# Gathered groups of a four-layer graph network: one matmul per edge column over the three bf16 parts side by side, summed by VectorE out of PSUM

## The chip, the cores and the metric

The kernel runs on one core of a Trainium2 chip. The metric is the time of one execution on the device in microseconds (us); lower is better. TensorE multiplies matrices into PSUM, VectorE does elementwise work and reductions, ScalarE activations, GpSimd (POOL) starts the indirect gathers, and SyncE (SP) starts the plain DMA transfers. [...]

## The reference

12500 nodes with 64 features, 200000 edges `src -> dst` sorted by `dst`, and four layers in a row, each followed by a residual and a layer norm:

```python
edge_index = jnp.stack([src, dst])
x = _layernorm(x + _L0_gnn_ref(x, edge_index, ...))            # graph attention, 4 heads
x = _layernorm(x + _L1_gnn_ref(x, edge_index))                 # standard deviation of the neighbours
x = _layernorm(x + _L2_gnn_ref(x, edge_attr_64, src, dst, ...))# messages with edge features, then an MLP
x = _layernorm(x + _L3_gnn_ref(x, edge_index, ...))            # four sage_conv in a row

def sage_conv(x, src, dst, Wl, bl, Wr):
    msg = x[src]
    agg = jax.ops.segment_sum(msg, dst, num_segments=N_NODES)
    deg = jax.ops.segment_sum(jnp.ones((src.shape[0], 1), x.dtype), dst, num_segments=N_NODES)
    agg = agg / jnp.maximum(deg, 1.0)
    return agg @ Wl.T + bl + x @ Wr.T
```

The core of each layer is a segment sum: for every node, the sum of the rows of its in-neighbours. The second layer needs the sums of x and of its square (128 columns), the four `sage_conv` those of 64, 32, 32 and 64 columns.

## The kernel before

Nodes are cut into 98 tiles of 128. There are seven passes over the graph: gat, dev, gine, sage1, sage2, sage3, sage4. Gat and gine gather every edge's row in f32. The other five (dev and the four sage passes) are "dense" passes with `parts` = 3: a float is split into three bf16 parts, which lie side by side in a table row of 3 x n columns (n = 128, 64, 32, 32, 64), and a sum over the three parts gives the f32 sum back.

A dense pass (`pass_dense`, once for TensorE and once for VectorE) sums in two ways:

- **Counted tiles.** For the first 49 destination tiles (KT = 49) the kernel has built, once, a matrix of edge counts per pair of tiles in DRAM (`counts`). `dense_unit` streams one destination tile's count blocks through the SBUF ring `RING` in pieces (`piece_loaded`, `piece_used`) and multiplies each 128x128 block with the rows of all source tiles, in two halves with a PSUM bank each (`ps_dense`): 98 matmuls a unit (in dev, whose tables are wider, the source tiles are taken in two sweeps, 49 matmuls a unit). Line 921 is that matmul; it already takes the three parts at once, 3 x n columns wide. VectorE's `take_dense` (lines 1740 to 1752) reduces the three parts out of PSUM into `DSUM` (L1746), waits for that reduce, and adds it to the accumulator (L1750).
- **Gathered groups.** The remaining edges, those of the higher destination tiles, are taken in 15 rounds per pass. A round (`cold_round`) has 8 slots, a slot is a group of 512 edges, 128 partitions by C = 4 edge columns. POOL gathers the rows of a slot with 4 indirect DMAs (L620) as soon as the slot's indices have been refilled (`take_indices`, L1695). A group touches one or more destination tiles t; each (group, tile) is a **pair**. For a pair VectorE writes a one-hot matrix of 128x512 (`hot`, L1700) into one of two buffers, and TensorE multiplies it with the gathered rows into one of two PSUM banks (`ps_pair`, L949): 4 edge columns times 3 parts, 12 matmuls of n columns that accumulate into the same n columns.

A gathered round is called from `cold_rounds` between two units; how many rounds stand behind which unit is a schedule computed on the chip (`TURNS`). The order on TensorE is written by hand: unit (both halves), then rounds, then the next unit. On VectorE it is `take_dense` of half 0, the rounds, `take_dense` of half 1.

Within a round the two engines run one pair apart. VectorE, for pair p: one-hot of p, wait for the matmuls of p-1 (`pair_agg`), add the sum of p-1 from PSUM to the accumulator of its tile (`add`, L1707), then swap the buffers. TensorE, for pair p: wait for the one-hot of p (`pair_hot`) and for the add of p-2 (`pair_acc`), which frees the PSUM bank. After every 7 units the last pair still in PSUM is added by `flush`, whose steps run on a chain semaphore (`step` waits for each), and then the node work of a block or two follows (`node_vector`, `node_tensor`: L1200, L685 and so on); TensorE goes on with the next unit afterwards.

`settle(eng)` is a semaphore increment that carries the wait ahead of it.

Of the kernel before, what the change touches and what calls it, by code (L numbers as in the profile page):

```python
# [25 lines left out]
C = 4  # L26
# [58 lines left out]
def build(nc, x, edge_attr, src_r, dst_r, dst_b, src_c, dst_c, w, out):  # L85
    ctx = ExitStack()
    with ctx:
        def sb(name, shape, dt=F32):
            return ctx.enter_context(nc.sbuf_tensor(name, shape, dt))

        def sem(name):
            return ctx.enter_context(nc.semaphore(name))
# [43 lines left out]
        xp_before = [sum(xp_loads[:k]) for k in range(len(passes))]  # L136

        table_done = sem("table_done")
        pair_hot, pair_agg, pair_acc = sem("pair_hot"), sem("pair_agg"), sem("pair_acc")
        piece_loaded = [sem(f"piece_loaded_{j}") for j in range(len(PIECES))]  # L140
        piece_used = [sem(f"piece_used_{j}") for j in range(len(PIECES))]
        xp_loaded, dense_read, dense_added = sem("xp_loaded"), sem("dense_read"), sem("dense_added")
# [94 lines left out]
        iota_f = arena(WIDE_ROW, at=5 * COLS + 4 * TB)  # L237

        DSUM = sb("DSUM", [P, 2, 2 * D])
        MOST = sb("MOST", [P, 2])  # L240
        FLAG = sb("FLAG", [P, 1])
        HOTS = sb("HOTS", [P, 2])
# [469 lines left out]
        def _(pe):  # L712
# [212 lines left out]
            def pass_dense(k):  # L925

                ps = passes[k]
                n, buf, row = ps["n"], ps["buf"], ps["row"]
                dev = ps["name"] == "dev"

                def cold_round(r):

                    pe.reg_add(arrived, arrived, 16 * C)
                    for s in range(SLOTS):
                        lo, hi = load_four(pe, spans, s, r * SLOTS + s)
                        pe.wait_ge(ps["gathered"][s], pe.snap(arrived, min_val=1, max_val=len(passes) * ROUNDS * 16 * C))
                        settle(pe)
                        with pe.Fori(lo, hi) as t:
                            pe.reg_add(seen, seen, 1)
                            count = pe.snap(seen, min_val=1, max_val=len(passes) * GROUPS * TILES)  # L940
                            pe.wait_ge(pair_hot, count)
                            settle(pe)
                            pe.wait_ge(pair_acc, count)
                            settle(pe)
                            hot = onehot_ring[:, bass.ds(pe.snap(turn, min_val=0, max_val=1024), GE)]
                            sums = ps_pair[:, bass.ds(pe.snap(bank, min_val=0, max_val=512), n)]
                            for c in range(C):
                                for q in range(3):
                                    last = pe.matmul(sums, hot[:, c * P:(c + 1) * P], buf[:, s, c, q * n:(q + 1) * n],  # L949
                                                     start=(c == 0 and q == 0), stop=(c == C - 1 and q == 2))  # L950
                            last.then_inc(pair_agg, 1)
                            pe.reg_alu(turn, turn, 1024, ALU.bitwise_xor)
                            pe.reg_alu(bank, bank, 512, ALU.bitwise_xor)

                r0 = pe.value_load(INFO[0:1, 0:1], min_val=0, max_val=ROUNDS - 1)
                if dev:
                    pe.wait_ge(chunk_read, CHUNKS + 2)
                    for q in range(2):
                        last = pe.matmul(ps_pair[:, 512 * q:512 * q + n], ZERO[:, :], ZEROS[:, 0:n], start=True, stop=True)
                    last.then_inc(pair_agg, 1)  # L960
                    for half in range(2):
                        pe.wait_ge(xp_loaded, 16 * (xp_before[k] + half + 1))
                        with pe.Fori(0, KT) as u:
                            dense_unit(k, u, u + half * KT, SRC_HALF)
                            if half == 0:
                                cold_rounds(pe, u, r0, cold_round)
                    return
                pe.wait_ge(xp_loaded, 16 * (xp_before[k] + xp_loads[k]))
                with pe.Fori(0, STEPS) as b:
                    with pe.Fori(0, TB) as r:  # L970
                        u = b * TB + r
                        dense_unit(k, u, u, TILES)
                        cold_rounds(pe, u, r0, cold_round)
                    node_tensor(pe, k, b * 2)
                    node_tensor(pe, k, b * 2 + 1)
# [275 lines left out]
        def _(ve):  # L1251
# [433 lines left out]
            def pass_dense(k):  # L1685
# [11 lines left out]
                def hot(cols, t):  # L1697
# [3 lines left out]
                                                   TBASE[:, bass.ds(t, 1)], COL[:, :].unsqueeze(1).broadcast_to([P, C, P]),  # L1701
                                                   ALU.subtract, ALU.is_equal)

                def add():

                    a = acc[:, bass.ds(ve.snap(prev, min_val=0, max_val=TILES), 1), :]
                    return ve.tensor_tensor(a, a, ps_pair[:, bass.ds(ve.snap(bank, min_val=0, max_val=512), n)].unsqueeze(1), ALU.add)  # L1707

                def cold_round(r):

                    for s in range(SLOTS):
                        g = r * SLOTS + s
                        lo, hi = load_four(ve, spans, s, g)
                        with ve.Fori(lo, hi) as t:  # L1714
                            ve.reg_add(pairs, pairs, 1)
                            count = ve.snap(pairs, min_val=1, max_val=len(passes) * GROUPS * TILES)
                            hot(g * C + C, t).then_inc(pair_hot, 1)
                            ve.wait_ge(pair_agg, count)
                            settle(ve)
                            ve.wait_ge(pair_acc, count)  # L1720
                            settle(ve)
                            add().then_inc(pair_acc, 1)
                            ve.reg_mov(prev, t)
                            ve.reg_alu(turn, turn, 1024, ALU.bitwise_xor)
                            ve.reg_alu(bank, bank, 512, ALU.bitwise_xor)
                        take_indices((s - 1) % SLOTS, g + (SLOTS - 1))

                def flush():

                    ve.reg_add(after, pairs, 1)  # L1730
                    count = ve.snap(after, min_val=1, max_val=len(passes) * GROUPS * TILES)
                    ve.wait_ge(pair_agg, count)
                    settle(ve)
                    ve.wait_ge(pair_acc, count)
                    settle(ve)
                    step(add())
                    settle(ve)
                    ve.reg_mov(prev, TILES)
# [23 lines left out]
                    take_indices(s, r0 * SLOTS + s)  # L1762
                if name == "dev":
                    with ve.Fori(0, STEPS) as b:
                        step.loop(b, per + 1)
                        with ve.Fori(0, TB) as r:
                            unit(b * TB + r, b * TB + r, True)
                        flush()
                        node_vector(ve, step, k, split, b, b + STEPS)
# [6 lines left out]
                    step.close(STEPS)  # L1776
                    return
                with ve.Fori(0, STEPS) as b:
                    step.loop(b, 2 * per + 1)
                    with ve.Fori(0, TB) as r:  # L1780
                        unit(b * TB + r, b * TB + r, True)
                    flush()
# [50 lines left out]
```

## Time and profile before

| | |
|---|---|
| median of 3 runs | 12794.58 us (12789.05 to 12804.66) |
| the profiled execution | 12813.53 us |
| its span on the core | 12811.7 us |
| mean granted TensorE clock | 0.668 of full speed |
| TensorE matmul busy | 7656.7 us (60%), 61727 matmuls |
| TensorE weight load busy | 5494.5 us (43%) |
| VectorE busy | 5118.7 us (40%) |
| ScalarE busy | 1761.8 us (14%) |
| POOL busy | 5615.3 us (44%) |
| passes with gathered groups of three parts | dev's from 5.86 ms, sage1 to sage4 from 9.2 ms to the end |

The busy shares are means over stages with different limits. PE is TensorE's matmul row, PEld its weight loads, DVE VectorE; an engine's name with a q behind it is its sequencer. An instruction is named by its line, as L949. "Idle before" is what the engine had no work for, and the arrow names what ended it; "issue" means that nothing in the profile did.

### The profile page before, as it was taken

How to read it: one execution, taken by the hardware profiler on the slowest of the kernel's cores; microseconds unless marked ns; L12 is line 12 of the kernel's file. 1: busy time of each engine (PE TensorE's matmuls, PEld its weight loads, DVE VectorE, ACT ScalarE, POOL GpSimd, SP SyncE). 2: the span in 40 equal slices, each digit the busy share in tenths (PEclk: the TensorE clock that was granted, in tenths of full speed). 3: DMA queues.
4: the chain of work that ended last, by engine and by line, in shares of the span. 5: the costliest groups of instructions: out<-in, count | busy, mean ns of one | idle time of the engine just before them, and what ended most of it. 6: DMA issues, size and time to landing. Idle time of an engine off the chain costs nothing.

```text
span 12811.7 us, 273411 instructions
## 1 busy us (share of the span) xinstructions
PE 7656.7 (60%) x61727; PEld 5494.5 (43%) x61728; DVE 5118.7 (40%) x13474; ACT 1761.8 (14%) x3566; POOL 5615.3 (44%) x5555
## 2 busy tenths in 40 slices
PE   5666666663665555556788444444566655455666
PEld 4555555552112222224455333444555544444566
DVE  4444545546544444443433222333322233322333
ACT  2333333331012222330000000000000000000000
POOL 4666555452000000005530577777654376554554
PEclk7777777776555555557889655566677766666777
DMA  2222222221001111115555322222455566655666
GB/s 59 66 63 63 64 62 61 61 59 36 20 40 54 66 70 70 70 80 169 150 169 176 75 51 56 56 58 58 121 189 173 198 206 232 217 183 199 203 216 202
DMA packets 977744, 1416.34 MB, mean 111 GB/s; under 512 B 540705, under 2 KB 649761, under 8 KB 970914
## 3 DMA queue, kind: packets, MB, share of 16 engines
q1 hardware_dynamic: 689858, 1130.79, 26.0%
q0 software_dynamic: 184832, 224.29, 9.0%
q10 hardware_dynamic: 102752, 58.62, 1.6%
q14 instruction: 281, 2.30, 0.1%
q8 instruction: 21, 0.34, 0.0%
HBM read 1197.73 MB, written 215.36 MB: 110 GB/s over the span
## 4 chain that ended last, share of the span: by engine, by line
PE 31%; issue 23%; DVE 14%; DVEq 14%; POOL 9%; DMA 6%; ACT 1%; SPq 1%; POOLq 0%; ACTq 0%
PE ps_turn L921 13%; POOL ARENA L620 9%; PE ps_turn L884 7%; PE ps_out L776 4%; DMA ARENA<-table_gat,idx 2%; DMA ARENA<-counts 2%; DVE onehots L1700 2%; DVEq L1714 2%; PE ps_pair L776 1%; DMA idx<-src_r 1%; DVEq L392 1%; PE ps_turn L692 1%; PE ps_pair L949 1%; DVE ARENA L1635 1%; DVEq L1630 1%
## 5 line engine op out<-in xcount | busy, mean ns | idle before, releaser
L620 POOL DMA_INDIRECT ARENA<-table_sage,idx x1920 | 1901.7, 990 | 1729.5 <-DVE idx L1695 1192.8
L921 PE MATMUL ps_turn<-ARENA 128*128 128x96 bf16 (+2 forms) x24010 | 2274.4, 262 | 543.0 <-DVE DSUM L1746 215.9
L921 PEld LDWEIGHTS ps_turn<-ARENA 128*128 128x128 bf16 x24010 | 1864.0, 106 | 948.7 <-issue 647.7
L884 PE MATMUL ps_turn<-ARENA 128*128 x3736 | 1515.8, 508 | 1219.5 <-issue 584.4
L620 POOL DMA_INDIRECT ARENA<-table_gat,idx x1568 | 1671.9, 1066 | 1188.1 <-issue 1131.0
L620 POOL DMA_INDIRECT ARENA<-table_gine,idx x1568 | 1541.2, 983 | 964.1 <-issue 950.1
L620 POOL DMA_INDIRECT ARENA<-table_dev,idx x480 | 481.8, 1004 | 2660.0 <-DVE idx L1695 2522.3
L1635 DVE TENSOR_SCALAR ARENA<-ARENA 128x784 f16 x1868 | 902.6, 483 | 1415.9 <-PE ps_turn L884 963.9
L949 PE MATMUL ps_pair<-ARENA,onehots 128*128 128x32 bf16 (+2 forms) x10140 | 699.7, 227 | 997.4 <-DVE ARENA L1707 868.6
L776 PE MATMUL ps_out<-ARENA,onehots 128*128 128x256 f32 (+1 forms) x3136 | 950.0, 472 | 517.7 <-DMA ARENA<-table_gine,idx 368.9
L884 PEld LDWEIGHTS ps_turn<-ARENA 128*128 x3736 | 389.1, 104 | 1959.0 <-issue 1863.2
L776 PE MATMUL ps_pair<-ARENA,onehots 128*128 128x256 f32 (+1 forms) x3136 | 882.5, 446 | 389.1 <-DMA ARENA<-table_gine,idx 303.4
L949 PEld LDWEIGHTS ps_pair<-ARENA,onehots 128*128 x10140 | 574.0, 117 | 1128.3 <-issue 1127.1
L776 PEld LDWEIGHTS ps_out<-ARENA,onehots 128*128 128x128 f32 x3136 | 724.1, 286 | 631.5 <-issue 555.5
L1073 ACT ACTIVATE ARENA<-ps_turn 128x784 f32 x784 | 645.4, 823 | 2112.9 <-PE ps_turn L902 2112.9
L1746 DVE TENSOR_REDUCE DSUM<-ps_turn 128x128 f32<-128x384 f32 (+2 forms) x588 | 230.0, 391 | 1756.2 <-PE ps_turn L921 1643.5
L1700 DVE SCALAR_TENSOR_TENSOR onehots<-DST,TBASE,COL 128x512 f32 x845 | 637.0, 754 | 640.0 <-issue 639.5
L776 PEld LDWEIGHTS ps_pair<-ARENA,onehots 128*128 128x128 f32 x3136 | 677.8, 269 | 493.9 <-issue 429.3
L1030 ACT ACTIVATE bigT<-ps_turn 128x896 f32<-128x896 f32 (+1 forms) x42 | 38.4, 915 | 3454.3 <-PE ps_turn L685 3454.3
L1450 DVE TENSOR_TENSOR ARENA<-ARENA,ps_out 128x261 f32 (+1 forms) x584 | 205.7, 354 | 761.8 <-PE ps_out L776 761.3
L1018 ACT ACTIVATE tmp<-COL,dst_in 128x128 bf16<-128x128 f32 x1568 | 495.3, 386 | 0.0
L776 PE MATMUL ps_out<-ARENA,tmp 128*128 128x256 f32 (+1 forms) x1536 | 417.2, 435 | 128.0 <-DVE tmp L1444 126.2
(298 smaller groups left out, 6850.4 us busy)
## 6 DMA issues: line engine op xcount, KB each, us to landing
ARENA<-counts SPq DMA_DIRECT2D x1470, 448.0 KB
counts<-ARENA SPq DMA_DIRECT2D x49, 3136.0 KB, 9.0
ARENA<-counts SPq DMA_DIRECT2D x490, 224.0 KB
ARENA<-dst_b SPq DMA_DIRECT2D x393, 256.0 KB
ARENA<-edge_attr SPq DMA_DIRECT2D x390, 128.0 KB, 2.5
ARENA<-table_sage,idx POOLq DMA_INDIRECT x1920
ARENA<-table_gat,idx POOLq DMA_INDIRECT x1568
ARENA<-table_gine,idx POOLq DMA_INDIRECT x1568
```

What stands on the lines that cost most here:

```text
L620: pool.indirect_dma_start(ps["buf"][:, s, c, 0:ps["row"]], None, ps["table"][:, :], bass.IndirectOffsetOnAxis(idx[:, s, c:c + 1], 0)).then ...
L776: last = pe.matmul(sums[:, 0:H * D if gat else n], lhs, rhs, start=(c == 0 and q == 0), stop=(c == C - 1 and q == parts - 1))
L884: last = pe.matmul(ps_turn[:, at:at + WIDE_ROW // 2], ring[:, 0:P], ring[:, P + q * (WIDE_ROW // 2):P + (q + 1) * (WIDE_ROW // 2)], start= ...
L921: last = pe.matmul(ps_dense[half][:, 0:n], RING[:, b, :], XP[:, b, :], start=(b == PIECE_AT[pieces[0]]), stop=(j == pieces[-1] and b == PI ...
L949: last = pe.matmul(sums, hot[:, c * P:(c + 1) * P], buf[:, s, c, q * n:(q + 1) * n], start=(c == 0 and q == 0), stop=(c == C - 1 and q == 2))
L1018: act.activation(distance[:, c * P:(c + 1) * P], COL[:, :], ACT.Abs, scale=-1.0, bias=dst_in[:, s % 2, c:c + 1]).then_inc(hot_distance, 1)
L1073: act.activation(to[:, :, c * CHUNK:(c + 1) * CHUNK].rearrange("p (q b) v -> p q b v", q=2), sums.rearrange("p q (b v) -> p q b v", v=CHUN ...
L1450: return ve.tensor_tensor(a, a, ps_sums[q][:, 0:n].unsqueeze(1), ALU.add)
L1635: ve.tensor_scalar(ring[:, P:P + WIDE_ROW], IOTA16, BASES[:, bass.ds(i * 4 + c, 1)], KEY[:, bass.ds(j, 1)], ALU.add, ALU.is_equal).then_in ...
L1700: return ve.scalar_tensor_tensor(ring, DST[:, bass.ds(cols, C)].unsqueeze(2).broadcast_to([P, C, P]), TBASE[:, bass.ds(t, 1)], COL[:, :].u ...
L1714: with ve.Fori(lo, hi) as t:
L1746: ve.tensor_reduce(DSUM[:, half, 0:n], ps_dense[half][:, 0:3 * n].rearrange("p (q v) -> p v q", q=3), X_AXIS, ALU.add).then_inc(dense_read, 1)
```

## The change

In `cold_round` of TensorE the inner loop over the three parts goes. One matmul per edge column takes the slot's whole row, 3 x n columns, into 3 x n columns of the PSUM bank (at most 384 of 512). VectorE gets a new step `join`, a reduce over the three parts out of PSUM into a new SBUF tile `PAIR_SUM`, with a semaphore `pair_sum` on which the add then waits; the add reads `PAIR_SUM`. The flush gets the same two steps, as two links of its chain. In dev the banks' opening with zeros covers all three parts.

```diff
@@ TensorE, cold_round
-                            sums = ps_pair[:, bass.ds(pe.snap(bank, min_val=0, max_val=512), n)]
+                            sums = ps_pair[:, bass.ds(pe.snap(bank, min_val=0, max_val=512), 3 * n)]
                             for c in range(C):
-                                for q in range(3):
-                                    last = pe.matmul(sums, hot[:, c * P:(c + 1) * P], buf[:, s, c, q * n:(q + 1) * n],
-                                                     start=(c == 0 and q == 0), stop=(c == C - 1 and q == 2))
+                                last = pe.matmul(sums, hot[:, c * P:(c + 1) * P], buf[:, s, c, :], start=(c == 0), stop=(c == C - 1))
                             last.then_inc(pair_agg, 1)
@@ TensorE, dev: the banks are opened with zeros
                     for q in range(2):
-                        last = pe.matmul(ps_pair[:, 512 * q:512 * q + n], ZERO[:, :], ZEROS[:, 0:n], start=True, stop=True)
+                        for part in range(3):
+                            last = pe.matmul(ps_pair[:, 512 * q + part * n:512 * q + (part + 1) * n], ZERO[:, :], ZEROS[:, 0:n], start=True, stop=True)
@@ VectorE
+        PAIR_SUM = sb("PAIR_SUM", [P, 2 * D])
+                def join():
+
+                    parts = ps_pair[:, bass.ds(ve.snap(bank, min_val=0, max_val=512), 3 * n)]
+                    return ve.tensor_reduce(PAIR_SUM[:, 0:n], parts.rearrange("p (q v) -> p v q", q=3), X_AXIS, ALU.add)
+
                 def add():

                     a = acc[:, bass.ds(ve.snap(prev, min_val=0, max_val=TILES), 1), :]
-                    return ve.tensor_tensor(a, a, ps_pair[:, bass.ds(ve.snap(bank, min_val=0, max_val=512), n)].unsqueeze(1), ALU.add)
+                    return ve.tensor_tensor(a, a, PAIR_SUM[:, 0:n].unsqueeze(1), ALU.add)
@@ VectorE, cold_round
                             ve.wait_ge(pair_acc, count)
                             settle(ve)
+                            join().then_inc(pair_sum, 1)
+                            ve.wait_ge(pair_sum, count)
+                            settle(ve)
                             add().then_inc(pair_acc, 1)
@@ VectorE, flush
                     ve.wait_ge(pair_acc, count)
+                    settle(ve)
+                    step(join())
                     settle(ve)
                     step(add())
```

## Rows read from the trace of the kernel before

**Rows 1.** The page: the chain that ended last, by engine and by line.
```profile
PE 31%; issue 23%; DVE 14%; DVEq 14%; POOL 9%; DMA 6%; ACT 1%; SPq 1%; POOLq 0%; ACTq 0%
PE ps_turn L921 13%; POOL ARENA L620 9%; PE ps_turn L884 7%; PE ps_out L776 4%; DMA ARENA<-table_gat,idx 2%; DMA ARENA<-counts 2%; DVE onehots L1700 2%; DVEq L1714 2%; PE ps_pair L776 1%; DMA idx<-src_r 1%; DVEq L392 1%; PE ps_turn L692 1%; PE ps_pair L949 1%; DVE ARENA L1635 1%; DVEq L1630 1%
```

**Rows 2.** Groups: busy us, mean ns, idle before; last, one line's shortest, median, longest.
```profile
L949 PE MATMUL ps_pair<-ARENA,onehots 128*128 128x32 bf16 (+2 forms) x10140 | 699.7, 227 | 997.4 <-DVE ARENA L1707 868.6
...
L949 PEld LDWEIGHTS ps_pair<-ARENA,onehots 128*128 x10140 | 574.0, 117 | 1128.3 <-issue 1127.1
...
L1700 DVE SCALAR_TENSOR_TENSOR onehots<-DST,TBASE,COL 128x512 f32 x845 | 637.0, 754 | 640.0 <-issue 639.5
...
L1707 DVE TENSOR_TENSOR ARENA<-ARENA,ps_pair x880: 173/214/290, 5857.4 to 12794.8; - x176
```

**Rows 3.** Timeline of PE, a round of sage1: start us, duration us, instruction, idle before.
```profile
9217.70 8.25 PE L921 MATMUL ps_turn<-ARENA 128*128 128x192 bf16 x98 [1.15 <-DVE DSUM L1746]
9227.99 0.65 PE L949 MATMUL ps_pair<-ARENA,onehots 128*128 128x64 bf16 x12 [2.04 <-DVE ARENA L1707]
...
9233.24 0.82 PE L949 MATMUL ps_pair<-ARENA,onehots 128*128 128x64 bf16 x12 [1.05 <-DVE ARENA L1707]
...
9246.33 0.82 PE L949 MATMUL ps_pair<-ARENA,onehots 128*128 128x64 bf16 x12 [0.76 <-DVE ARENA L1707]
9248.31 9.75 PE L921 MATMUL ps_turn<-ARENA 128*128 128x192 bf16 x98 [1.16 <-issue]
```

**Rows 4.** Timeline of DVE in the same round.
```profile
9229.04 0.22 DVE L1707 TENSOR_TENSOR ARENA<-ARENA,ps_pair  x1 [0.61 <-PE ps_pair L949]
9229.97 0.75 DVE L1700 SCALAR_TENSOR_TENSOR onehots<-DST,TBASE,COL 128x512 f32 x1 [0.71 <-issue]
9230.86 0.22 DVE L1707 TENSOR_TENSOR ARENA<-ARENA,ps_pair  x1
...
9231.95 0.82 DVE L1700 SCALAR_TENSOR_TENSOR onehots<-DST,TBASE,COL 128x512 f32 x1 [0.22 <-issue]
...
9232.69 0.21 DVE L1707 TENSOR_TENSOR ARENA<-ARENA,ps_pair  x1
```

**Rows 5.** The reduce L1746 in dev, sage1 and sage2: ns shortest/median/longest.
```profile
L1746 DVE TENSOR_REDUCE DSUM<-ps_turn x192: 557/558/559, 5852.5 to 7112.8; 128x128 f32<-128x384 f32 x192
...
L1746 DVE TENSOR_REDUCE DSUM<-ps_turn x98: 357/358/359, 9195.6 to 10165.4; 128x64 f32<-128x192 f32 x98
...
L1746 DVE TENSOR_REDUCE DSUM<-ps_turn x98: 257/258/259, 10209.0 to 10962.6; 128x32 f32<-128x96 f32 x98
```

**Rows 6.** Waits of DVE over the whole kernel: us in total, times, longest us.
```profile
DVE ARENA L1707 <- PE ps_pair L949: 115.0, 137, 2.7
```

**Rows 7.** Timeline of DVE: the add behind a reduce.
```profile
9254.78 0.28 DVE L1750 SCALAR_TENSOR_TENSOR ARENA<-DSUM,FLAG,ARENA 128x64 f32 x1 [0.26 <-DVE DSUM L1746]
```

**Rows 8.** Timelines of DVE and of PE around a flush in sage1.
```profile
9770.25 0.28 DVE L1750 SCALAR_TENSOR_TENSOR ARENA<-DSUM,FLAG,ARENA 128x64 f32 x1 [0.16 <-DVE DSUM L1746]
9771.33 0.22 DVE L1707 TENSOR_TENSOR ARENA<-ARENA,ps_pair  x1 [0.80 <-DVE ARENA L1750]
9772.03 0.63 DVE L1200 TENSOR_TENSOR big<-ARENA,RDEG 128x448 f32 x1 [0.47 <-DVE ARENA L1707]
...
9773.61 1.73 PE L685 MATMUL ps_turn<-IDENT,big 128*128 128x128 f32 x7 [3.60 <-DVEq L1202]
```

**Rows 9.** Windows: PE, PEld, DVE, ACT, POOL busy; PE clock, DMA share, GB/s.
```profile
5858.00:5880.00 22.00, 14.37 (x132) 11.62 (x132) 11.87 (x28) 0.00 (x0) 16.82 (x18) 0.59 0.34 99
9228.00:9247.00 19.00, 8.50 (x132) 7.02 (x132) 10.74 (x28) 0.00 (x0) 14.40 (x15) 0.58 0.32 96
```

**Rows 10.** Timeline of PE: a burst in dev and one in sage2.
```profile
5859.83 1.46 PE L949 MATMUL ps_pair<-ARENA,onehots 128*128 128x128 bf16 x12 [0.89 <-DVE ARENA L1707]
...
10248.28 0.65 PE L949 MATMUL ps_pair<-ARENA,onehots 128*128 128x32 bf16 x12 [1.15 <-DVE ARENA L1707]
```

**Rows 11.** The costliest groups: the gathers of the sage passes.
```profile
L620 POOL DMA_INDIRECT ARENA<-table_sage,idx x1920 | 1901.7, 990 | 1729.5 <-DVE idx L1695 1192.8
```

More of the change, by code:

```diff
@@ L138, in build @@
         table_done = sem("table_done")
-        pair_hot, pair_agg, pair_acc = sem("pair_hot"), sem("pair_agg"), sem("pair_acc")
+        pair_hot, pair_agg, pair_sum, pair_acc = sem("pair_hot"), sem("pair_agg"), sem("pair_sum"), sem("pair_acc")
         piece_loaded = [sem(f"piece_loaded_{j}") for j in range(len(PIECES))]
@@ L1764, in pass_dense @@
                     with ve.Fori(0, STEPS) as b:
-                        step.loop(b, per + 1)
+                        step.loop(b, per + 2)
                         with ve.Fori(0, TB) as r:
@@ L1778, in pass_dense @@
                 with ve.Fori(0, STEPS) as b:
-                    step.loop(b, 2 * per + 1)
+                    step.loop(b, 2 * per + 2)
                     with ve.Fori(0, TB) as r:
```

## The prediction

> **What bounds the kernel now.** I began with the chain of work that ended last [rows 1]: no engine owns it. TensorE has 31% of the span, time in which nothing shown was waited for 23%, VectorE 14% and its sequencer another 14%. L1714, the pair loop's head on VectorE's sequencer, stands there with 2% and L1700 (the one-hot) with 2%, while L949, the matmuls that the change rewrites, has 1%. Then the costliest groups [rows 2]: L949 is 10140 matmuls, and 10140 / 12 = 845 pairs, as many as L1700 ran; 845 / 5 passes = 169 pairs a pass. L1707, the add, ran 880 times: 845 pairs and 5 x 7 flushes.
>
> The timeline of TensorE shows where the pairs lie [rows 3]. Counted and gathered work alternate strictly: a unit of 98 counted matmuls, then a gathered round (units are 98 matmuls, in dev 49). I counted 75 rounds, 15 a pass, of 10 to 12 pairs. In the one shown a burst of 12 matmuls takes 0.65 to 0.82 us, and the next begins about 1.8 us after it: (9246.33 - 9227.99) / 10 = 1.83 us a pair. TensorE is idle for more than half of the round, and its clock stands mostly at the lower level (0.58 over this round) [rows 9]. Unit and round are not overlapped on TensorE, so what lengthens a round lengthens the pass.
>
> What sets the 1.8 us is on VectorE [rows 4]. The one-hot takes 0.75 us; the add of the pair before follows at its end (9231.95 to 9232.69), or later where it waits for TensorE (the 0.61 us idle before 9229.04); the next one-hot starts 0.93 to 1.09 us after the add started, and VectorE's engine is idle for much of that: its sequencer is working through registers, the loop's branch and the next address. So VectorE as a whole, engine and sequencer, is the loop, and TensorE runs in its shadow. The wait of L1707 for L949 sums to 115.0 us in 137 cases over the whole kernel [rows 6].
>
> **The change, part by part.**
>
> *Matmuls.* 10140 become 3380, but the streamed columns stay: 12 x 128 = 4 x 384. A burst of the dev pass takes 1.46 us at the lower clock [rows 10]; 1536 columns at 1.2 GHz are 1.28 us, the rest is the tail of the last matmul. Nothing is gained there, nor at 64 columns (768 / 1.2 GHz = 0.64 us of 0.82). At 32 columns 12 matmuls take 0.65 us, 54 ns each [rows 10], and 4 x 96 columns at 1.2 GHz are 0.32 us and a tail: I take 0.14 us off the burst. A burst lies beside the next one-hot, so little of this counts.
>
> *The reduce (new).* The same instruction on the same shapes exists in take_dense: 558, 358 and 258 ns for 384, 192 and 96 inputs [rows 5]. It can't start before the one-hot that is ahead of it in VectorE's queue has ended, exactly where the add stands now.
>
> *The wait on the reduce (new).* The add now waits for pair_sum, settles and computes its address. take_dense has the same sequence, and VectorE is idle between reduce and L1750 for 0.26 us [rows 7] or 0.16 us [rows 8]; I take 0.21. While it waits, VectorE's sequencer is stopped, so the loop's branch, take_indices and the next one-hot all stand behind it, and TensorE's next burst waits for that one-hot. Nothing covers it. The add itself, now from SBUF, isn't waited for before the next one-hot; whatever it gains or loses counts nothing.
>
> *Sum in the rounds.* The first burst of a round needs only its one-hot, which is ahead of the reduce; 169 - 15 = 154 pairs a pass pay. One dev pass, two of 64 columns, two of 32: 154 x (0.77 + 2 x 0.57 + 2 x 0.47) = 437 us.
>
> *What comes back.* Where the add now waits for TensorE, a longer loop lets the burst finish in time; at most the 115 us of rows 6. Not all: the wait at the second pair of a round (the 0.61 us of rows 4) stays, since TensorE enters the round late, after its unit. I carried all 845 pairs through with the distances of rows 3 and 4: an add or reduce starts at the later of the one-hot's start + 0.67 and the burst's end + 0.40 us; a one-hot starts its own measured distance after the add; a burst starts 0.47 us after its one-hot's end (9231.95 + 0.82 to 9233.24) or its own measured distance after the burst before. Unchanged, this gives the present rounds back within 1 us in all. With reduce and wait put in it gives +87 (dev), +68, +62, +63 and +70 us: **+350**, so 87 of the 437 come back. Without the shorter bursts at 32 columns it is 358.
>
> *Flushes.* Before a block's node work the flush adds the last pair, and the node work (L1200, then TensorE's L685) stands right behind it [rows 8]; the step chain makes it wait for the reduce too. 7 a pass, each the reduce and about 0.25: 5.7 + 8.5 + 7.1 = **+21** us.
>
> *Clock.* In the dev pass part of the rounds still runs at 2.4 GHz (0.59 as mean in one of them [rows 9]). With TensorE idler, more of it may fall; carried through with every burst at the lower clock the rounds cost **+4** us more. In the later passes the clock is at the lower level for most of a round already.
>
> *Hidden.* Gathers: POOL's gathers for the four sage tables stood idle 1192.8 us for VectorE's freed indices [rows 11], so later rounds delay nothing. The DMA engines are busy for 0.32 to 0.34 of a round [rows 9], so the pieces of counts have long been refilled when it ends, and a longer round gives the next unit nothing. Four more zeroing matmuls in dev are nothing.
>
> Sum: 350 + 21 + 4 = 375. The profiled execution took 12813.5 us (span 12811.7), the median of the runs is 12794.6, 0.15% less; put on the median, 12794.6 + 375 = **13170 us**.
>
> The bounds: with 0.15 us for the wait and all 115 us back, 391 - 115 + 18 = 294, 13089 us; with 0.26 us and nothing back, 476 + 24 + 9 = 509, 13304 us.
>
> [...]
>
> **Rivals.**
> 1. *TensorE's waits come back in full, and the wait is short.* Speaks for it: 137 waits that a slower loop should remove. Against: those at the second pair stay. About 13090 us.
> 2. *The stopped sequencer costs more.* The sequencer now prepares a part of the loop under the one-hot; with two more address computations and a semaphore wait 0.26 us or more, nothing recovered: 13300 us or above.
> 3. *Weight loads were on the path.* LDWEIGHTS of L949 are 574.0 us busy [rows 2]; two thirds gone are -383. If each stood in line ahead of its matmuls and in the loop, 437 + 21 - 383 = +75: 12870 us. Against it: the burst lies beside a 0.75 us one-hot, and L949 has 1% of the chain.
> 4. *TensorE's issue sets the pair, and it gets faster.* Its sequencer issues 24 instructions a pair, then 8, and in 65% of the pairs (counted over all 845) the burst starts over 0.5 us after the one-hot's end, so TensorE is late by its own work. If VectorE had as much slack as the reduce takes, the gain would be that of the replay with bursts of 0.3 us and no reduce: -123, 12672 us. It decides only if reduce and wait cost under 123 / 770 = 0.16 us on the path; the reduce alone is 0.26 at the least.
>
> **Chances.** My forecast 0.78; rival 1: 0.08; rival 2: 0.08; rival 3: 0.03; rival 4: 0.03. About 0.2% (26 us) is what a measurement of this kernel can tell from no change. Faster by more than that is rival 4, 0.03; within it 0.01, a mixture of 3 and 4; slower 0.96. The range, 13085 to 13300, is that of the bounds above and leaves out rivals 3, 4 and a part of 2 and 1.
>
> **What would show it.** Right: join's reduce 880 times at about 560, 360 and 260 ns; 3380 matmuls at L949's place; a round of the first sage pass at 23 to 24 us instead of 19.2, of dev at 27 to 28, of 32 columns at 23; dense units unchanged, 8.25 us for 98 at the full clock; L1707's wait for TensorE down from 115 to 30-50 us. Wrong: if the next one-hot starts sooner after the add than 0.93 to 1.09 us, because the sequencer was held by the engine there and not by its own work; if the units after a round get slower through the clock; if bursts of 4 wide matmuls take longer than those of 12.

## The result and the profile after

The changed kernel takes 13201.02 us (median of 4 runs, 13193.15 to 13218.30), the kernel before 12792.9 us: ratio 1.0319, 95% interval 1.0301 to 1.0337. That is 408 us slower; 375 were forecast, and 13201 lies in the range of 13085 to 13300. In later runs the same pair gave 13214.58 against 12820.38 us, ratio 1.0301 (1.0284 to 1.0319).

The page of the changed kernel, the two groups of L949 (TensorE's matmuls of the pairs and their weight loads), to be held against [rows 2]. L922 is the counted matmul, L1707 the new reduce, L1712 the add, L1756 and L1760 the two steps of take_dense.

```profile
L949 PE MATMUL ps_pair<-ARENA,onehots 128*128 128x96 bf16 (+2 forms) x3380 | 729.5, 343 | 1345.0 <-DVE onehots L1700 1198.6
...
L949 PEld LDWEIGHTS ps_pair<-ARENA,onehots 128*128 x3380 | 363.8, 108 | 1702.7 <-issue 1631.2
```

A third of the matmuls are left, and they are busy for 729.5 us instead of 699.7: the columns are the same. TensorE now waits for the one-hot (L1700) before 775 of the 845 bursts (1198.6 us); in the kernel before it was the add (L1707) before 748.

The timeline of TensorE over the first sage1 round, to be held against [rows 3]:

```profile
9315.84 0.80 PE L949 MATMUL ps_pair<-ARENA,onehots 128*128 128x192 bf16 x4 [2.02 <-DVE ARENA L1712]
...
9339.24 0.82 PE L949 MATMUL ps_pair<-ARENA,onehots 128*128 128x192 bf16 x4 [1.42 <-DVE onehots L1700]
```

A burst of 4 x 192 columns takes 0.82 us, as one of 12 x 64 did. The round has 11 pairs as in the rows before and now takes 9340.06 - 9315.84 = 24.2 us, where it took 19.2. VectorE in the same round, against [rows 4]:

```profile
9320.93 0.75 DVE L1700 SCALAR_TENSOR_TENSOR onehots<-DST,TBASE,COL 128x512 f32 x1 [0.17 <-issue]
9321.60 0.35 DVE L1707 TENSOR_REDUCE PAIR_SUM<-ps_pair 128x64 f32 x1
9322.21 0.22 DVE L1712 TENSOR_TENSOR ARENA<-ARENA,PAIR_SUM 128x64 f32 x1 [0.26 <-DVE PAIR_SUM L1707]
9322.75 0.17 DVE L1695 CAST idx<-ARENA 128x4 int32 x1 [0.32 <-issue]
9323.31 0.75 DVE L1700 SCALAR_TENSOR_TENSOR onehots<-DST,TBASE,COL 128x512 f32 x1 [0.39 <-issue]
```

The reader is to see the reduce in the add's old place (0.67 us after the one-hot's start), the add 0.61 us behind it, and then 1.10 us to the next one-hot (L1695, which takes the next slot's indices, lies in between). One turn, from a one-hot to the next, is 2.38 us. In the kernel before that last distance was not always 1.1 us. Where the add didn't have to wait for TensorE it was shorter, as in these lines of the same round of the kernel before (9241.45 - 9240.58 = 0.87 us):

```profile
9239.91 0.75 DVE L1700 SCALAR_TENSOR_TENSOR onehots<-DST,TBASE,COL 128x512 f32 x1 [0.39 <-issue]
9240.58 0.21 DVE L1707 TENSOR_TENSOR ARENA<-ARENA,ps_pair  x1
9240.89 0.17 DVE L1695 CAST idx<-ARENA 128x4 int32 x1
9241.45 0.75 DVE L1700 SCALAR_TENSOR_TENSOR onehots<-DST,TBASE,COL 128x512 f32 x1 [0.39 <-issue]
```

The waits of VectorE in the whole changed kernel, against [rows 6]:

```profile
DVE ARENA L1712 <- DVE PAIR_SUM L1707: 228.7, 880, 0.3
...
DVE PAIR_SUM L1707 <- PE ps_pair L949: 17.2, 19, 2.0
```

I added up all 75 rounds in both traces (first burst's start to last burst's end) and what lies between the first and the last round of each pass:

| | before | after | difference |
|---|---|---|---|
| rounds of dev | 330.2 | 424.0 | +93.8 |
| rounds of sage1 | 295.4 | 372.0 | +76.6 |
| rounds of sage2 | 292.2 | 359.4 | +67.2 |
| rounds of sage3 | 294.1 | 357.9 | +63.7 |
| rounds of sage4 | 296.5 | 373.1 | +76.6 |
| all rounds | 1508.4 | 1886.4 | +377.9 |
| between rounds, five passes | 2668.7 | 2694.5 | +25.8 |
| span | 12811.7 | 13206.9 | +395.2 |

So 378 of the 395 us between the two traces arose inside the rounds. The other 8.5 us, by which the span grew less than rounds and stretches together, lie where no round runs: 5.6 ahead of the first round, 4.1 between dev and sage1, 1.2 back at the other places.

The 770 turns inside the rounds (154 in each pass), added up in their parts, show where it arose:

| us, sum of 770 turns | before | after | difference |
|---|---|---|---|
| one-hot's start to the start of what follows it (add, now reduce) | 697.8 | 536.3 | -161.6 |
| reduce's start to the add's start | 0 | 469.9 | +469.9 |
| add's start to the next one-hot's start | 797.7 | 870.8 | +73.1 |
| all | 1495.6 | 1877.0 | +381.4 |

At the earliest an add or reduce starts 0.67 us after its one-hot. In the kernel before 488 of the 770 adds started later, as a rule 0.42 us after the end of TensorE's burst; that is what the 161.6 us are. It is more than the 115.0 us of [rows 6], which hold only 137 of these cases. The second pair of traces gives the same parts to within 4 us.

### The profile page after: what moved, and what is told of

The parts are those of the page before. It is cut to its first block, busy times and chain, and to the rows that moved or that the text cites. A ratio compares the mean times of both kernels' runs of the same rounds, so it can differ in the third digit from the quotient of the medians.

```text
span 13206.9 us, 262222 instructions
## 1 busy us (share of the span) xinstructions
PE 7683.4 (58%) x54971; PEld 5286.2 (40%) x54972; DVE 5394.9 (41%) x14354; ACT 1762.7 (13%) x3566; POOL 5566.1 (42%) x5555
## 4 chain that ended last, share of the span: by engine, by line
PE 29%; issue 25%; DVE 15%; DVEq 14%; POOL 9%; DMA 6%; ACT 1%; SPq 0%; POOLq 0%; ACTq 0%
PE ps_turn L922 12%; POOL ARENA L621 9%; PE ps_turn L885 7%; PE ps_out L777 4%; DVE PAIR_SUM L1707 2%; DMA ARENA<-table_gat,idx 2%; DVEq L1719 2%; DMA ARENA<-counts 2%; PE ps_pair L777 1%; DMA idx<-src_r 1%; DVE ARENA L1635 1%; DVEq L393 1%; PE ps_turn L693 1%; DVEq L1630 1%; PE ps_out L697 1%
## 5 line engine op out<-in xcount | busy, mean ns | idle before, releaser
L621 POOL DMA_INDIRECT ARENA<-table_sage,idx x1920 | 1873.7, 976 | 2052.3 <-DVE idx L1695 1550.4
L922 PE MATMUL ps_turn<-ARENA 128*128 128x96 bf16 (+2 forms) x24010 | 2275.9, 262 | 550.4 <-DVE DSUM L1756 280.8
L922 PEld LDWEIGHTS ps_turn<-ARENA 128*128 128x128 bf16 x24010 | 1866.0, 106 | 967.1 <-issue 665.7
L949 PE MATMUL ps_pair<-ARENA,onehots 128*128 128x96 bf16 (+2 forms) x3380 | 729.5, 343 | 1345.0 <-DVE onehots L1700 1198.6
L949 PEld LDWEIGHTS ps_pair<-ARENA,onehots 128*128 x3380 | 363.8, 108 | 1702.7 <-issue 1631.2
L1756 DVE TENSOR_REDUCE DSUM<-ps_turn 128x128 f32<-128x384 f32 (+2 forms) x588 | 229.9, 391 | 1733.4 <-PE ps_turn L922 1608.8
L1700 DVE SCALAR_TENSOR_TENSOR onehots<-DST,TBASE,COL 128x512 f32 x845 | 637.0, 754 | 661.0 <-issue 660.6
```

Source lines behind the costliest of these rows:

```text
L621: pool.indirect_dma_start(ps["buf"][:, s, c, 0:ps["row"]], None, ps["table"][:, :], bass.IndirectOffsetOnAxis(idx[:, s, c:c + 1], 0)).then ...
L922: last = pe.matmul(ps_dense[half][:, 0:n], RING[:, b, :], XP[:, b, :], start=(b == PIECE_AT[pieces[0]]), stop=(j == pieces[-1] and b == PI ...
L1700: return ve.scalar_tensor_tensor(ring, DST[:, bass.ds(cols, C)].unsqueeze(2).broadcast_to([P, C, P]), TBASE[:, bass.ds(t, 1)], COL[:, :].u ...
L1756: ve.tensor_reduce(DSUM[:, half, 0:n], ps_dense[half][:, 0:3 * n].rearrange("p (q v) -> p v q", q=3), X_AXIS, ALU.add).then_inc(dense_read, 1)
```

## Experiments

The kernels ran on different chips. On one chip every kernel behaved as in the runs above (the kernel before 12817 to 12820 us); on two others the kernel before itself took 16128 to 16136 us. Ratios are always to the kernel before on the same chip. What is seen of the second setting is taken up in its own part; I call it the stalled setting. Edits are against the changed kernel, if nothing else is said, and are shown shortened, with several lines of the kernel in one.

### Reduce run, but not waited for

```diff
-  join().then_inc(pair_sum, 1); ve.wait_ge(pair_sum, count); settle(ve)
+  join().then_inc(pair_sum, 1)
   add().then_inc(pair_acc, 1)      # reads ps_pair[bank], n columns, as in the kernel before
```

The flush goes back to its form before. The add takes only the first part, so two of three parts are missing from the gathered sums.

> The changed kernel with the reduce, but the add doesn't wait for it and reads the first part's columns from PSUM; the two other parts' sums are left out of the result. The reduce is still run 845 times. Theory (what costs is that VectorE's sequencer stands while the reduce runs, so that branch and next address come behind it): most of the 408 us goes, 60 to 130 us above the kernel before are left for the dispatch of one more instruction (12850 to 12920). Rival (the reduce's own time on VectorE's engine costs): its 275 us in the rounds stay, 13050 or more.

> The kernel of e4 again (reduce run, not waited for, the add reads the first part's columns and leaves two parts out), for a setting without the instruction stalls, in which the first answer can't be compared with the 408 us. Theory (the sequencer's stop behind the reduce is the price): ratio 1.005 to 1.010 to the kernel before, so 60 to 130 us more. Rival (the reduce's time on VectorE's engine is the price): 1.018 or more. If the stalls are back: 0.988, as before.

Without stalls: 12843.93 us against 12816.81, ratio 1.0021 (1.0011 to 1.0031). Only 27 us are left of some 400, less than either expectation. The rounds sum to 1539.5 us against 1504.6 in an unchanged kernel before on that chip. VectorE's timeline in a sage1 round, at one of its shorter turns:

```profile
9222.81 0.75 DVE L1700 SCALAR_TENSOR_TENSOR onehots<-DST,TBASE,COL 128x512 f32 x1 [0.36 <-issue]
9223.47 0.35 DVE L1707 TENSOR_REDUCE PAIR_SUM<-ps_pair 128x64 f32 x1
9223.74 0.21 DVE L1712 TENSOR_TENSOR ARENA<-ARENA,ps_pair  x1
9223.88 0.17 DVE L1695 CAST idx<-ARENA 128x4 int32 x1
9224.43 0.75 DVE L1700 SCALAR_TENSOR_TENSOR onehots<-DST,TBASE,COL 128x512 f32 x1 [0.38 <-issue]
```

The same reduce is there, but this turn is 1.62 us; the median turn of sage1 is 1.86 us, that of the kernel before 1.83, that of the changed kernel 2.37. In the sum of the 770 turns the reduce still puts the add off by 214 us. Against that the next one-hot starts 97 us sooner after the add than in the kernel before, and 86 us of waiting for TensorE come back; 31 us are left.

Why the next one-hot comes sooner is in the steps of VectorE's sequencer (DVEq), among them the loop's branch (L1719) and the address of the next index copy (L1695). In the same turn they begin while the engine reduces (9223.47 to 9223.82):

```profile
9223.49 0.07 DVE PAIR_SUM L1707
9223.56 0.03 issue
9223.59 0.04 DVEq L1719
9223.63 0.03 issue
9223.66 0.04 DVEq L1719
9223.71 0.04 issue
9223.74 0.09 DVEq L1695
```

In the changed kernel, in the turn shown above, they come behind the reduce and the add's address (L1711):

```profile
9321.60 0.36 DVE PAIR_SUM L1707
9321.96 0.03 issue
9321.99 0.02 DVEq L382
9322.01 0.07 issue
9322.08 0.07 DVEq L1711
...
9322.44 0.04 DVEq L1719
9322.49 0.03 issue
9322.52 0.04 DVEq L1719
9322.56 0.04 issue
9322.60 0.10 DVEq L1695
```

Over the 770 turns 2894 sequencer steps began while a reduce ran, among them the loop's branch in 290 turns; in the changed kernel not one did, and the branch came 0.57 us (median) behind the reduce's end. So what costs is that the sequencer stands until the reduce is over; without the wait the reduce's time on VectorE's engine cost nearly nothing (27 us). With stalls the same kernel was faster than before, 0.9884 (0.9858 to 0.9910).

### All of the computation, the add one pair later

```diff
   hot(g * C + C, t).then_inc(pair_hot, 1)
+  ve.wait_ge(pair_acc, count); settle(ve)     # both waits stood behind pair_agg
+  ve.wait_ge(pair_sum, count); settle(ve)
+  add(prev2, older).then_inc(pair_sum, 1)     # the sum reduced one turn ago
   ve.wait_ge(pair_agg, count); settle(ve)
-  ve.wait_ge(pair_acc, count); settle(ve)
-  join().then_inc(pair_sum, 1); ve.wait_ge(pair_sum, count); settle(ve)
-  add().then_inc(pair_acc, 1)
+  join().then_inc(pair_acc, 1)                # into the other of two buffers
+  ve.reg_mov(prev2, prev); ve.reg_alu(older, older, 128, ALU.bitwise_xor); ve.reg_alu(slot, slot, 128, ALU.bitwise_xor)
```

The flush adds two pairs now, and the registers get their first values (left out here).

> All of the computation, with the add put off by one pair: one-hot of p, add of the reduced sum of p-2, wait for the matmuls of p-1, reduce of p-1 into the other of two buffers; the reduce is never waited for at once, but the loop has one more wait and two more register steps, about 0.3 us of sequencer time a pair. Theory (the stop of the sequencer is the price): clearly below the changed kernel, by 120 to 220 us, about 13030 us. Rival (the reduce's engine time is the price): within 50 us of the changed kernel.

> The kernel of e3 again (all of the computation, the add one pair later so that the reduce is never waited for at once), without the stalls. Theory: 120 to 220 us below the changed kernel, ratio 1.014 to 1.022 to the kernel before; rival: within 50 us of the changed kernel, 1.027 or more. If the stalls are back: 1.000, as before.

Without stalls: 13007.12 us, ratio 1.0153 (1.0135 to 1.0171), 207 us below the changed kernel on the same chip (13214.58, in an earlier series there). The output is the full one, so half of the change's loss was the order of VectorE's steps. The other half isn't taken apart: the rounds are 143 us longer than in the kernel before (1647.7 against 1504.6; a turn of 2.13 us in a sage1 round), the stretches between them, where each flush has another add, 64 us. The extra wait and register steps are the likely cause in the rounds; no run isolates them. With stalls it equalled the kernel before, 0.9998 (0.9982 to 1.0014).

### The reduce twice

```diff
+  join(PAIR_TWICE)                 # a spare tile
   join().then_inc(pair_sum, 1)
   ve.wait_ge(pair_sum, count)
```

> The changed kernel with the reduce of every pair in the rounds run twice, the first time into a spare tile; one wait behind both. Theory (VectorE's loop sets the pair and nothing hides the reduce): without stalls the changed kernel plus 154 x (0.56 + 2 x 0.36 + 2 x 0.26) = 277 us, less up to 20 for what TensorE's waits still give back. Rival (the wait costs and the reduce is mostly hidden): under 100 us more.

13440.98 us, ratio 1.0481 (1.0464 to 1.0499): 226 us above the changed kernel (13214.58), 31 less than the least that was expected (257). The rival is out. The rounds grew by 74 us in dev, 43 and 41 at 64 columns, 25 and 24 at 32, so by 0.48, 0.27 and 0.16 us a pair, 0.07 to 0.10 less than a reduce. The timeline shows why:

```profile
9422.91 0.35 DVE L1708 TENSOR_REDUCE PAIR_TWICE<-ps_pair 128x64 f32 x1
9423.18 0.35 DVE L1708 TENSOR_REDUCE PAIR_SUM<-ps_pair 128x64 f32 x1
9423.78 0.23 DVE L1713 TENSOR_TENSOR ARENA<-ARENA,PAIR_SUM 128x64 f32 x1 [0.25 <-DVE PAIR_SUM L1708]
```

The second starts 0.08 us before the first has ended, which the expectation had left out. From the first reduce to the add the 770 turns now hold 675.4 us instead of 469.9, 205 more: the added reduces are 270 us, the overlaps 64. The rounds grew by 206 in all. So nothing but this overlap was hidden: with a wait behind the reduce, its whole time was on the path. No run has the wait without the reduce.

### The changed and the unchanged kernel again

> The kernel before, unchanged, for its trace in the setting of the first four runs, in which every kernel took some 26% longer than in the runs shown. If that setting holds again: 16135 us, and TensorE's sequencer shows register steps and branches of about 0.7 us between the matmuls of a burst, where the trace of before shows some 0.05 us. If not: 12795 us and none of them.

> The changed kernel, unchanged. Where instructions come without stalls: ratio 1.032, as measured. Where TensorE's sequencer stalls for its instructions: theory (the stalls make a burst of 12 cost several us, and the change spares TensorE 16 of 24 instructions a pair, which pays for most of the reduce and the wait): ratio 0.995 to 1.015. Rival (the stalls fall on VectorE's loop as well, and its longer loop costs more than TensorE saves): 1.03 or more.

Both without stalls: 12815.46 and 13214.58 us. The rounds sum to 1504.6 and 1887.2 us, those of the runs shown to 1508.4 and 1886.4, so the two sets of runs agree to within 4 us there. The question of the stalled setting was not answered by them.

### The matmuls alone, and the reduce with narrow matmuls

```diff
 # the matmuls alone: no join, no pair_sum, the add reads ps_pair[bank], n columns (two parts are left out)
 # narrow: TensorE's inner loop of the changed kernel becomes
+  for q in range(3):
+      last = pe.matmul(ps_pair[:, bass.ds(bank + q * n, n)], hot[:, c * P:(c + 1) * P],
+                       buf[:, s, c, q * n:(q + 1) * n], start=(c == 0 and q == 0), stop=(c == C - 1 and q == 2))
```

The narrow form isn't the inner loop of the kernel before: `bank` is a register, and each of the 12 matmuls computes its own address in PSUM, a register step per matmul, where the kernel before and the changed one have three register steps in a burst.

> The matmul half of the change alone: 4 wide matmuls, no reduce and no new wait; the add reads the first part's columns from PSUM and leaves the two other parts' sums out. Theory: only the shorter bursts at 32 columns count, 5 to 15 us less than the kernel before (12780 us). Rival (TensorE's issue sets the pair): about 120 us less, 12670. Rival (weight loads on the path): up to 380 us less.

> The matmul half of the change alone again (4 wide matmuls, no reduce, no new wait, the add reads the first part's columns only and leaves two parts out), without the stalls. Theory: 5 to 15 us less than the kernel before, ratio 0.999. Rival (issue or loads of TensorE on the path): 60 us less or more, 0.995 or below. With stalls: 0.986, as before.

> The changed kernel with its reduce and wait, but with 12 narrow matmuls a pair again, each part summed into its own n columns of the bank. Theory (VectorE's loop sets the pair, the burst lies beside the one-hot): the time of the changed kernel, 0 to 15 us above it, so 13200 to 13215 us, ratio to the kernel before 1.031 to 1.034. Rival (the number of loads or of issued instructions counts, and the wide matmuls give back a part of the price): 60 us or more above the changed kernel, up to 120.

> The changed kernel with reduce and wait, but 12 narrow matmuls a pair, again, without the stalls. Theory: 0 to 15 us above the changed kernel, ratio 1.030 to 1.034 to the kernel before. Rival: 60 us or more above it, 1.036 or more. With stalls: 1.022, as before.

All four fell into the stalled setting. The matmuls alone: 15905.36 and 15896.43 us, ratios 0.9862 (0.9836 to 0.9888) and 0.9858 (0.9832 to 0.9884), as two chips agree. Narrow matmuls with reduce and wait: 16476.60 and 16463.33 us, 1.0220 (1.0190 to 1.0249) and 1.0201 (1.0168 to 1.0234). There the wide matmuls are worth 231 us (16127.73 - 15896.43). The register steps between TensorE's matmuls, in ns shortest/median/longest, show what differs. First the kernel before without stalls:

```profile
L949 PEldq FUSED_REGOPS  x2535: 46/46/56, 5863.6 to 12795.1; - x195
```

Then the matmuls alone, stalled, and the narrow form with its 10140 steps instead of 2535:

```profile
L949 PEldq FUSED_REGOPS  x2535: 2/46/1409, 6496.2 to 15894.8; - x195
...
L950 PEldq FUSED_REGOPS  x10140: 2/53/1420, 6523.5 to 16454.8; - x199
```

Then a wide burst on TensorE's timeline, stalled, in pieces:

```profile
10945.00 0.32 PE L949 MATMUL ps_pair<-ARENA,onehots 128*128 128x192 bf16 x1 [4.84 <-issue]
10946.41 0.48 PE L949 MATMUL ps_pair<-ARENA,onehots 128*128 128x192 bf16 x2 [1.08 <-issue]
```

And a burst with narrow matmuls:

```profile
11092.27 1.77 PE L950 MATMUL ps_pair<-ARENA,onehots 128*128 128x64 bf16 x12 [1.27 <-DVE ARENA L1714]
```

A register step that takes 0.05 us otherwise takes up to 1.4 us: 249 of the 2535 took over 0.3 us (these 0.70 in the median), none in the kernel before. The median stays 0.05, and the median wide burst of 192 columns 0.82 us; single bursts fall apart (the longest wide one took 5.2 us, the longest narrow one 8.0). VectorE's sequencer shows the same in the matmuls alone (the steps of L1700 2/105/1411 ns). The engines' own work isn't slower: the one-hot's median is 752 ns without stalls and 751 with them.

The 1.8 us of a narrow burst are another matter. The median is 1.85, 1.80 and 1.77 us at 128, 64 and 32 columns, and the matmuls start 0.13 to 0.16 us apart, each behind its own register step of 0.05 us. So it is the edit's nine added steps, and not the setting, that make the narrow burst long, and the two runs with the narrow form don't tell what 12 matmuls of the old form cost beside the reduce.

That the stalled setting makes TensorE's issue a part of the path, so that fewer instructions pay there, fits the 231 us; the kernel before has no trace in that setting. That the sequencers wait for their instructions at those places, as the expectation of the changed kernel has it, was my guess: no run shows what a long step waits for, nor whether the chip or the time made the setting. What the matmuls alone give without stalls wasn't measured; the bound is the kernel with the reduce not waited for, which has the wide matmuls too and ended 27 us above the kernel before. The changed kernel itself wasn't run in the stalled setting.

### The kernel before, the add's address computed ahead of the wait

```diff
-  ve.wait_ge(pair_agg, count); settle(ve)
   ve.wait_ge(pair_acc, count); settle(ve)
-  add().then_inc(pair_acc, 1)
+  a, sums = operands()             # the add's addresses
+  ve.wait_ge(pair_agg, count); settle(ve)
+  add(a, sums).then_inc(pair_acc, 1)
```

> The kernel before with VectorE's two waits of a pair exchanged and the add's address computed ahead of the wait for TensorE's matmuls; no instruction is added or dropped. Theory (in the kernel before, half of the pairs wait for TensorE and the sequencer's work behind that wait is on the path): without stalls 25 to 50 us less than the kernel before, ratio 0.996 to 0.998; with stalls of TensorE, which make VectorE wait longer, as much or more, 0.993 to 0.998. Rival (those steps are hidden by the one-hot): no change.

This is the kernel before with VectorE's waits exchanged: 12790.34 us against 12820.38, ratio 0.9975 (0.9965 to 0.9984), 30 us less, as expected. The rounds sum to 1485.4 us, 19 less than in the unchanged kernel's trace on that chip. The adds that waited for TensorE started 0.28 us after the burst's end (median), those of the kernel before 0.42: the address work behind that wait was on the path there. It is a gain of a quarter of a per cent.

## Why the prediction was right, and its terms

The price of reduce and wait was right, and so was the place where it is paid. The rest of the sum came out by luck: two terms were wrong by 75 and 73 us and cancel. What then is left of the miss is mostly the wait that was taken too short.

- **The bound.** VectorE's engine and sequencer together are the pair loop. Shown by the reduce twice (only the overlap hidden) and by the reduce not waited for (27 us left). From the add's start to the next one-hot's the sequencer's steps, registers, branch and address, fill 0.61 of 0.93 us in the kernel before (7 steps) and 0.74 of 1.10 us in the changed one (9 steps; medians of the 770 turns).
- **Reduce.** Read from L1746 as 558, 358 and 258 ns; the shortest and longest of L1707 in dev, and its median of 550 (350 and 250 in sage1 and sage2), are up to 13 ns below:

```profile
L1707 DVE TENSOR_REDUCE PAIR_SUM<-ps_pair x176: 545/550/558, 5851.8 to 6751.1; 128x128 f32 x176
```

- **The reduce's start.** It was to start no sooner than the one-hot's end, where the add stands. Both start before that end: the reduce by 0.083 us (median of the 770 turns), the add of [rows 4] at 9232.69, where the one-hot ends at 9232.77.
- **Wait.** Taken as 0.21 us, measured 228.7 / 880 = 0.26, the longer of the two rows I had. Over 770 pairs that is 38 us too little. With the measured durations the price before anything comes back is 154 x (0.81 + 2 x 0.61 + 2 x 0.51) = 470 us, not 437; the turns show 469.9. That the sequencer is stopped meanwhile was right: in none of the 770 turns does a step of it begin while the reduce runs, and the first comes 0.04 us behind its end.
- **What comes back.** I gave 87 us and held 115 for the most there was. 162 came back. [rows 6] count only idle time of the engine that is put down to TensorE, 137 cases, where 488 adds started late. I also said that the wait at a round's second pair stays. A quarter of it does: at that place the adds were late by 76 us in all, the reduces are by 19, and VectorE's waits for L949 fell to 17.2 us (30 to 50 were forecast). The first turn of a round now has the reduce and its wait too, which delays the second one-hot until the first burst is nearly over (one-hot at 9316.31, burst over at 9316.64, reduce at 9317.00).
- **The next one-hot.** I kept its measured distance from the add, that is, put any change of it at nothing. It grew by 73 us in all, from 1.04 to 1.13 us on average. In the 282 turns of the kernel before in which the add followed the one-hot at once, the distance was 0.94 us; in the same turns of the changed kernel it is 1.15. In the others it was 1.09 and is 1.12. So where the sequencer had handed the add over in time, a part of its work for the next turn lay under the one-hot (its first step began before the one-hot's end in 338 of the 770 turns); behind the wait for the reduce it never does (0 of 770). That is the mechanism of rival 2, beside a return that rival 2 had denied.
- **The sum.** 470 - 162 + 73 = 381, and the rounds, counted from burst to burst, grew by 378. Forecast were 437 - 87 + 0 = 350 and 4 for the clock.
- **The bounds.** The upper one adds 24 for the flushes, where its 0.26 us give 22, and 9 for the clock without a working; 115 us as the most that can come back, in the lower one, was no bound.
- **Matmuls.** No gain at 128 and 64 columns, as said. The 0.14 us at 32 columns didn't come: the median burst is 0.643 us, before it was 0.649, though four matmuls of 96 columns take 0.32 at the 0.080 us from start to start that the counted ones of that width have at the lower clock. In both kernels the edge columns of a burst start 0.129 us apart (median), each behind a register step, with one wide or three narrow matmuls. The forecast had put 8 us on the shorter burst, inside its 87. The prediction's 1.2 GHz is the pace in the trace at a granted clock of 0.50: matmuls of 128 columns start 0.107 us apart there, those of 64 columns 0.053, so 1.2 columns a ns. At a granted clock of 1.00 the counted matmuls of 384 and 192 columns start 0.162 and 0.082 us apart, 2.3 to 2.4 columns a ns; that is the prediction's 2.4 GHz. What it calls the tail is in the record of a dev burst's last matmul, 0.31 us long: twelve starts 0.107 us apart are 1.28 us, the burst 1.46.
- **Clock.** It fell more than I looked for: over the 15 dev rounds the mean granted clock was 0.69 before and is 0.53, and 15 of the 169 bursts are as short as at the higher level (under 1.3 us; the others take 1.46), where 69 were. It costs next to nothing in the rounds, since VectorE seldom waits for a burst any more; the last bursts of the dev rounds, which end them, grew by 1.2 us in all. The 4 us were not measured as a term of their own.
- **Flushes.** 21 forecast. From the end of take_dense's add to the end of the flush's add the 35 flushes take 56.6 us, before 36.7: 20 more. The stretches between rounds grew by 25.8 in all. The dense units at the full clock still take 8.24 us.
- **The signs.** A round of 11 pairs takes 27.6 us in dev, 24.1 and 24.3 at 64 columns, 23.2 and 23.1 at 32 (medians), as forecast. Of the signs of being wrong none came; the next one-hot did move, but away from the add and not towards it.
- **Loads.** The short bursts aren't set by their loads: 0.649 us with twelve, 0.643 with four. The median load takes 114 ns before and 105 after; within an edge column of 32-column matmuls, those of the kernel before, each with its load, start 0.03 to 0.05 us apart, so the loads overlap. Rivals 3 and 4 (12870 and 12672 us) are out without stalls; in the stalled setting issue by TensorE seems to count, as rival 4 would have it, for another reason than the one it named.

## What to carry to other kernels

Before moving work from an engine that waits to one that others wait for, look at what its sequencer does between two instructions: a dependent pair with a wait between them cost the first one's duration here, the gap of 0.26 us, and the sequencer's work behind it that used to run under the engine (73 us). What a row of waits shows as idle time can be less than what a slower loop gets back (115 against 162 us here); add up the distances between the instructions instead. If such a step is needed, let its result be used one turn later; here that took away half of the loss. And put the wait for another engine as late as it can stand, with addresses computed ahead of it (30 of 12820 us here).

## What the runs showed of the hardware

- With no wait between them VectorE's instructions overlapped by 0.08 us here: the 845 second reduces started 0.083 us before the first had ended (median), the reduces of the changed kernel as much before the one-hot's end. With a wait 0.26 us of idle time lie between a reduce and its add.
- With one register step ahead of each edge column the columns start 0.129 us apart in the passes with n = 32, whether one wide or three narrow matmuls follow (bursts of 0.64 and 0.65 us). Twelve matmuls of 32 columns with a step each take 1.77 us (in the stalled setting, median). So at these widths the steps, and not the columns, set the burst.
- The kernel before took 12.8 ms on one chip and 16.1 ms on two others; in the kernels traced there the engines' durations were the same, and sequencer steps took up to 1.4 us. What a change is worth can differ between the two: the kernel with the reduce not waited for was at 1.0021 and 0.9884, the one with the late add at 1.0153 and 0.9998.
